# A graph layer in 41 steps instead of 45: 24 dense and 16 gathered tiles in each, count columns placed by each tile's span

## The reference, cut to what matters

```python
h = relu(layernorm(x))
deg = max(count of edges per dst, 1)
w_edge = (deg[src] * deg[dst]) ** -0.5
edge_msg = relu(edge_attr @ W1e + b1e) @ W2e + b2e          # edge_attr: (206250, 64)
agg = segment_sum((h[src] + edge_msg) * w_edge[:, None], dst)
combined = (1 + gin_eps) * h + agg
out = relu(combined @ W1n + b1n) @ W2n + b2n + h
return x + out * rsqrt(mean(out * out) + 1.19e-7) * rms_w
```

## Time and profile before

| | before |
|---|---|
| median of 3 runs | 1078.37 us (1076.29 to 1084.59) |
| the profiled execution | 1070.17 us, its span 1068.3 us |
| PE busy | 956.5 us, 90% |
| weight loads (PEld) | 765.3 us, 72% |
| DVE busy | 914.1 us, 86% |
| ACT busy | 651.4 us, 61% |
| POOL busy | 746.8 us, 70% |
| mean granted clock of PE | 0.993 |
| HBM | 147.95 MB read, 145 GB/s |

### The profile page before, as it was taken

How to read it: one execution, slowest core, us unless ns; L and a number is a source line. 1 busy time by engine, 2 the same in 40 slices (tenths; PEclk the granted TensorE clock), 3 DMA queues, 4 the chain that set the end, 5 groups by cost and what they waited for, 6 DMA issues and landing times. The chain is left out here.

```text
span 1068.3 us, 35619 instructions
## 1 busy us (share of the span) xinstructions
PE 956.5 (90%) x12753; PEld 765.3 (72%) x12753; DVE 914.1 (86%) x4066; ACT 651.4 (61%) x1747; POOL 746.8 (70%) x754
## 2 busy tenths in 40 slices
PE   0333999999999999999999999999999999999985
PEld 0332787887887887777887887787777788788753
DVE  6998988988988988988988988987887898898668
ACT  7972666666665665666666666666566666566435
POOL 2035777777777777777777777777777777777374
PEclk9999999999999999999999999999999999999988
DMA  6035455455554454455454455454455545452473
GB/s 240 15 147 202 145 150 141 139 153 143 142 156 143 138 161 143 133 163 144 123 173 140 129 172 136 131 163 130 141 147 150 143 140 157 141 135 67 157 299 106
DMA packets 57740, 156.99 MB, mean 147 GB/s; under 512 B 16051, under 2 KB 23398, under 8 KB 57184
## 3 DMA queue, kind: packets, MB, share of 16 engines
q1 hardware_dynamic: 33776, 104.43, 29.1%
q0 software_dynamic: 22784, 47.07, 18.8%
q10 hardware_dynamic: 1008, 3.21, 0.9%
HBM read 147.95 MB, written 6.70 MB: 145 GB/s over the span
## 5 line engine op out<-in xcount | busy, mean ns | idle before, releaser
L1065 POOL DMA_INDIRECT arena<-node_rows,idx x712 | 702.3, 986 | 228.9 <-issue 153.3
L1236 ACT ACTIVATE arena<-bank 128x294 f16<-128x294 f32 x900 | 327.2, 420 | 256.2 <-PE bank L1141 239.3
L1226 ACT ACTIVATE arena<-bank 128x512 f32<-128x512 f32 x405 | 222.6, 596 | 105.9 <-PE bank L1091 99.6
L1151 PE MATMUL bank<-t_words,arena 128*128 128x256 f16 x2205 | 276.2, 272 | 0.4 <-DVE arena L1354 0.4
L1291 DVE TENSOR_SCALAR arena<-iota_c,code 128x294 f16<-128x294 f16 x900 | 273.7, 359 | 2.3 <-PE bank L1141 2.3
L1304 DVE SCALAR_TENSOR_TENSOR arena<-iota_h,hi_f,bank 128x49 f32<-128x49 f32 x900 | 184.0, 260 | 77.6 <-PE bank L1106 75.7
L1141 PE MATMUL bank<-arena 128*128 128x294 f16 x900 | 206.2, 307 | 18.8 <-DVE arena L1291 12.4
L1091 PEld LDWEIGHTS bank<-w1e,arena 64*128 64x128 f32 x3240 | 215.6, 190 | 4.7
L1091 PE MATMUL bank<-w1e,arena 64*128 64x128 f32 x3240 | 218.1, 272 | 0.0
L1151 PEld LDWEIGHTS bank<-t_words,arena 128*128 128x128 f16 x2205 | 199.0, 97 | 21.2 <-issue 0.6
L1141 PEld LDWEIGHTS bank<-arena 128*128 128x128 f16 x900 | 101.4, 144 | 83.2 <-issue 37.1
(11 more groups left out here) (210 smaller groups left out, 804.9 us busy)
## 6 DMA issues: line engine op xcount, KB each, us to landing
arena<-in_attr SPq DMA_DIRECT2D x90, 512.0 KB
arena<-low_src SPq DMA_DIRECT2D x47, 652.5 KB, 7.6
arena<-node_rows,idx POOLq DMA_INDIRECT x712
arena<-in_attr SPq DMA_DIRECT2D x45, 128.0 KB
node_rows<-arena SPq DMA_DIRECT2D x1, 3160.5 KB, 8.9
arena<-in_x ACTq DMA_DIRECT2D x7, 448.0 KB, 10.9
arena<-in_x SPq DMA_DIRECT2D x6, 512.0 KB, 12.6
out<-arena SPq DMA_DIRECT2D x12, 224.0 KB
```

Source lines behind the costliest of these rows:

```text
L1065: nc.gpsimd.indirect_dma_start(out=edge_rows[:, u, j, 0:ROW], out_offset=None, in_=table, in_offset=bass.IndirectOffsetOnAxis(ap=idx[:, c, ...
L1151: mm = nc.tensor.matmul(x_sum[:, 0:2 * D], strip[:, u, k, :], T16[:, k, :], start=k == 0, stop=k == NBLK - 1)
L1226: nc.scalar.activation(out.rearrange("p (j o) d -> p o j d", o=2), z[:, :, j0:j0 + n // 2, :], ACT.Relu).then_inc(r_ready, 1)
L1236: nc.scalar.activation(strip[:, u, :, tile * W:tile * W + W], pair_bank[:, j * 512:j * 512 + CW].rearrange("p (k w) -> p k w", w=W), ACT.C ...
```

## The change

**Steps.** `TD` goes from 20 to 24: a step holds 24 dense and 16 gathered tiles, and 41 steps hold the 1612 tiles. There are 10 groups of four, two in each phase. The window is 112 nodes wide for the dense part and 88 for the gathered one.

**Columns.** 24 tiles of six columns would need 144, and a matmul has 128 rows. A tile now takes as many columns of `strip` as it spans targets. POOL works out the starts in the prologue: span of each tile, a running sum over 24, correction, two matrices of 41x984 that PE turns (4 matmuls) and DVE makes into a correction `off[:, 0]` with three operations of 128x984. ACT still writes six columns per tile; the tile after it writes over the surplus, so copies must land in order. Where they go is no longer fixed: ACT loads the starts of a phase's tiles into registers, two loads per phase and two for a step's first pair.

**Places.** In a phase PE counts `FIRST_PAIR[p]`, then the pairs in `MORE_PAIRS[p]`; where there are two of these, the first stands between two halves of the spread. ACT copies the first pair's counts between the two relus. The 49 blocks of the spread are dealt to the phases as 10, 4, 17, 17 and 1. `low_oh` is made for six tiles at a time, four times a step. Row buffers are laid as row, r, row, with one r between two rows.

```diff
-TD, TG = 20, 16
+TD, TG = 24, 16
-LOOKS = [0, 2, 4, 6, 8, 10]
+LOOKS = [0, 2, 4, 6, 9, 12]
-PHASES = [(0, 1), (2, 3), (4, 5), (6, 7), (8,)]
+PHASES = [(0, 1), (2, 3), (4, 5), (6, 7), (8, 9)]
-SPREAD_AT = [0, 10, 12, 27, 42, 49]
+SPREAD_AT = [0, 10, 14, 31, 48, 49]
+FIRST_PAIR = [1, 3, 5, 8, 11]
+MORE_PAIRS = [(2,), (4,), (6, 7), (9, 10), ()]
-LB = 10
+LB = 6
...
+            for by in (1, 2, 4, 8, 16):
+                nc.gpsimd.tensor_copy(widths[:, 1 - a, 0:by], widths[:, a, 0:by])
+                step(nc.gpsimd.tensor_tensor(widths[:, 1 - a, by:TD], widths[:, a, by:TD], widths[:, a, 0:TD - by], ALU.add))
...
+            pool.wait_ge(fast_ready, 1)
...
+            for a, of in ((0, starts[:, 1:TD + 1]), (1, jumps[:, :])):
+                nc.gpsimd.tensor_tensor(spread_out[:, a, :, :], own_step, of.unsqueeze(1).broadcast_to((S, S, TD)), ALU.mult).then_inc(columns_ready, 1)
...
+                    pool.wait_ge(deg_done, 1)
+                    pool.wait_ge(split_in, 16 * 12)
+                    nc.gpsimd.memset(strip_words, 0.0).then_inc(strip_clear, 1)
...
+            v.wait_ge(columns_turned, 1)
+            step(nc.vector.tensor_scalar(passed, bank2[0][:, 0:S * TD], part_f[:, 0:1], None, ALU.is_le))
+            step(nc.vector.tensor_tensor(passed, passed, bank2[1][:, 0:S * TD], ALU.mult))
+            step(nc.vector.tensor_reduce(off[:, 0, :], code[:, :, :], AX.X, ALU.add))
...
             def keep_counts(c, u, p):
                 for j in range(2):
                     act.wait_ge(tile_ps, 2 * (c * NA + p) + (j + 1))
+                    if p > 0:
+                        act.wait_ge(strip_ready, 2 * (c * NA + p - 1) + (j + 1))
-                    nc.scalar.activation(strip[:, u, :, tile * W:tile * W + W],
+                    nc.scalar.activation(strip[:, u, :, bass.ds(column_of[2 * p + j], W)],
...
-                        if p > 0:
-                            keep_counts(c, u, 2 * p)
-                        relu(c, u, 2 * p)
-                        if p < NPH - 1:
-                            relu(c, u, 2 * p + 1)
-                        keep_counts(c, u, 2 * p + 1)
+                        for q in MORE_PAIRS[p - 1] if p > 0 else ():
+                            keep_counts(c, u, q)
+                        load_columns(c, (FIRST_PAIR[p],) + MORE_PAIRS[p])
+                        relu(c, u, PHASES[p][0])
+                        keep_counts(c, u, FIRST_PAIR[p])
+                        relu(c, u, PHASES[p][1])
+                if live(c + 1):
+                    load_columns(c + 1, (0,))
```

More of the change, by code:

```diff
@@ L405, in degree_pass @@
                 mm.then_inc(placed, 1)
+            pe.wait_ge(columns_ready, 2)
+            for a in range(2):
+                numbers_of = spread_out[:, a, :, :].rearrange("p s t -> p (s t)")
+                for n0 in range(0, S * TD, 512):
+                    n1 = min(S * TD, n0 + 512)
+                    mm = nc.tensor.matmul(bank2[a][:, n0:n1], ones[0:S, :], numbers_of[:, n0:n1], start=True, stop=True)
+            mm.then_inc(columns_turned, 1)
             pe.wait_ge(zeros_ready, 1)
@@ L907, in look_of, with phase_of @@
 def look_of(pair):
-    return pair // UL * NPH + pair % UL // 2 + 1
+    return pair // UL * NPH + phase_of(pair % UL) + 1
+def phase_of(k):
+    return sum(k >= first for first in LOOKS[1:])
 def low_set(c, p):
@@ L925, in steps, with encode @@
         one(c, c % 2)
-def encode(nc, part, code, hi_f, rel_d, inside, step):
+def encode(nc, part, code, hi_f, rel_d, wide, inside, step):
     if part == 0:
@@ L934, in encode @@
     if part == 1:
-        step(nc.vector.scalar_tensor_tensor(out=inside, in0=rel_d[:, :, :], scalar=float(W), in1=inside, op0=ALU.is_lt, op1=ALU.mult))
+        step(nc.vector.scalar_tensor_tensor(out=inside, in0=rel_d[:, :, :], scalar=wide[:, 0:1], in1=inside, op0=ALU.is_lt, op1=ALU.mult))
     if part == 2:
@@ L1202, in one @@
                         turn(c - 1)
-                    if live(c) and not last:
-                        count_pair(c, u, 2 * p + 2)
+                    if more:
+                        count_pair(c, u, more[-1])
                     if live(c + 1) and last:
@@ L1227, in relu, with load_columns @@
                                      ACT.Relu).then_inc(r_ready, 1)
+            column_of = {}
+            def load_columns(c, pairs):
+                for j in range(2):
+                    at = j * NA + pairs[0]
+                    _, values = nc.values_load_multi_w_load_instructions(
+                        column_at[c:c + 1, at:at + len(pairs)], engines=(act.engine,), min_val=0, max_val=XS - W,
+                        skip_runtime_bounds_check_because="the prologue takes these columns only where the last one is at most XS - W")
+                    for p, value in zip(pairs, values):
+                        column_of[2 * p + j] = value
             def keep_counts(c, u, p):
@@ L1455 @@
     tile_of_slot = tiles(TILE_D + TILE_G)
-    group_of_slot = tiles([GROUP_AT[g] for g, _ in SLOTS_D] + [TD + GROUP_G[g] for g, _ in SLOTS_G])
     part = _np.arange(128)
```

285 lines of the change are left out of this document (180 added, 105 removed).

## The result

| | before | changed |
|---|---|---|
| median | 1078.23 us (1076.29 to 1084.59) | 1122.59 us (1121.18 to 1122.74) |
| ratio, 95% interval | | 1.0391 [1.0354, 1.0428] |
| span of the profiled execution | 1068.3 us | 1121.0 us |

The change makes the kernel 4% slower. The forecast was 1076 us, and 1122.6 lies outside its range. Of the rivals the third comes nearest: "at 0.25 per phase the step is 23.0 and the total +42".

A forecast was written before the change was run, and what follows sets the result against it. PE was taken to bound the steps, DVE next. Steps -11.3, prologue +7.0, head +3.9, tail and epilogue +0.2 made -0.2 against the profiled 1070.17; from the median 1078.37, less 2 us of lag: 1076 us, range 1061 to 1091.

The forecast's parts named there:

- third rival: ACT's register loads delay each phase's relu; decides from 0.5 us per step, total 1118 or 1092 us; chance 0.08.
- PE's step: Steady step on PE: 20.13 us plus 1.71 of work, -0.2 DVE waits, +0.3 ACT waits, making 21.94.
- DVE's work: Steady step on DVE: 17.5 us grows to 20.5, plus about 0.7 of waits for looks, staying behind PE.
- the lag of POOL: Steady steps: POOL's gathers get a step 1.8 us longer, so their lag and 3.4 us over 44 steps go.
- second rival: DVE becomes the bound, keeping 1.7 us of look waits beside 20.5 of work: step 22.2, total 1090; chance 0.10.
- so I cost them at 0: ACT's 12 register loads per step, issued during a 0.74 us wait for PE: 0; uncovered, up to 3.6 us.
- Copies at 0.73 a pair: ACT's copies of counts in a step: two more pairs, each taking 0.73 us as before the change.
- room on average: ACT in a step: busy 12.4 us grows to 14.4 of some 22, tight only inside phases 2 and 3.
- +0.3 for the middle and last pairs in phases 2 and 3: PE waits there for ACT's copies to free banks: +0.3 us per step, bounds 0 and 0.6.
- Head: First step, bound by DVE, and run-up picking four more tiles in series with looks: +3.9 us, 2 to 5.
- Prologue: DVE's chain: mask delay +4.2, three operations +3.2, longer operations +0.8, degrees -1.2: +7.0 us, 3 to 11.
- The 2 us: Plain runs exceed the profiled execution partly through lagging gathers; that lag goes, taking 2 us off the forecast total.

The follow-up runs named there:

- constant even columns: Changed kernel with dense column starts as even constants in the program, no loads or register operations on ACT, counts in wrong columns: 1081.54 us, ratio 1.0017.

## Why the prediction was wrong, point by point

- **PE's step** came out right, in part by luck. With ACT's two new costs taken away it is 22.03 for 21.94. In that kernel PE is busy 195.58 of 202 us, 21.33 a step where the kernel before has 19.91: +1.42 for the forecast +1.71. Its idle time rose by 0.4 where -0.2 and +0.3 were forecast. The two errors cancel.

```profile
326.00:528.00 202.00, 195.58 (x2779) 160.46 (x2780) 186.72 (x911) 129.58 (x340) 154.26 (x141) 1.00 0.50 145
```

- **DVE's work** (20.5) and the lag of POOL were right. DVE is busy 179.26 / 202 x 22.98 = 20.4 us a step. POOL is no longer full and waits for counts, 43.3 us of 400. PE's waits for DVE's pairs are off the list. DVE's waits for looks did not shrink to 0.7 but are 42.3 of 400 us, 2.4 a step; with constant even columns 28.1, or 1.55. In that kernel 20.4 and 1.55 fill 21.9 of 22.03 us, so whether PE or, as the second rival had it, DVE bounds it is open.
- **"so I cost them at 0"** is the step that failed. The loads were priced at the 303 ns of the earlier trace rows, a load of one value; here 8 of 12 fetch two or three values and take about 500 and 720 ns. Twelve are 6.1 us of ACT's queue, not the 3.6 named as the most. And the cover was one wait of 0.74 us in one phase, applied to all five; phases 2 and 3 load six values, 1.45 us. The register operations were put at nothing too, as covered by the copy before. Price of both: 0.69 us a step, 0.53 with even columns. The third rival, with a chance of 0.08, had its point of decision right, 0.5 us a step, but not its size: 0.25 in each of five phases would be 1.25 and make 23.2, not 23.0. The rule that spoke against the loads, a floor of about 600 ns per load (the Trainium skill, DMA: Bandwidth & Descriptors, "Latency and other measured facts"), is contradicted by the loads of 279 ns; its sum of 7.2 us came out near 6.1 for another reason, the number of values.
- **Copies at 0.73 a pair**: this duration belongs to even columns. The change moves where they land, and the mean rose from 420 to 503 ns. Price: 0.42 us a step, 0.26 without the loads. No rival had it.
- **"room on average"** for ACT compared 14.4 us of busy time with 22, and left the queue's own work out. With it ACT's sum is 22.6 of 22.98.
- **+0.3 for the middle and last pairs in phases 2 and 3** was of the right kind, but sat in the wrong place: PE's recorded waits are for the second relu of phases 1 and 4, at the head of phases 2 and 0, 8.2 us of 400. They come from the order and not from the two costs: with constant even columns they are 8.1.
- **Steps in all**: loads and odd columns together 0.95 x 40 = 38.0 of the 41.6 us missed; the other 3.6 are 0.09 a step.
- **Head**, 5.7 for 3.9: the same two costs. With constant even columns it is 142.7 - 106.4 = 36.3, only 2.7 more than before.
- **Prologue**, 16.0 for 7.0. The check's outcome (`fast`) is there 5.63 us later, 30.36 for 24.73, since `heads` arrives at 16.03 for 9.86. DVE waits 4.86 more for the mask. These were together to cost 4.2. Degrees gave back 1.4 (forecast 1.2). L691 lost 2.92 to the memset, which was costed at nothing ("releases nothing that is needed then"): the lock was overlooked. The three operations and the longer ones came as forecast, 3.2 and 0.8. The sum, 5.63 + 4.86 - 1.4 + 2.92 + 3.2 + 0.8, is 16.0. Why `heads` comes late stays open: with `tails` issued later its cast still started at 15.79. The new load of `slots`, 12.8 KB, took until 12.84 and was not tried at another place.
- **The 2 us** put into the forecast for lag in the plain runs: the guess had the right direction and was too small. Where the kernel before takes 1078 us, its runs spread over 8 to 16 us in each batch (1070.05 to 1086.09 in that of the constant even columns), and the changed kernel's over 1.6; ten runs with constant even columns lie within 0.9. So what makes most runs of the kernel before longer than the profiled one is gone with the change. What it is stays open, since only the one execution of 1070.17 us was traced.
- **3.4 us** "by which 888.9 exceeds 44x20.13" is 3.2; nothing hangs on it.

With both costs gone the kernel ties with the median of the one before (1.0017), but only because most plain runs of that one are slower than its profiled run. Against the profiled execution of the kernel before its span is 11.5 us longer: four steps fewer save 7.7, and prologue, head and tail cost 16.0, 2.7 and 0.5. No version that computes the layer beats the kernel before.

## What to carry to other kernels

Count an engine's queue work (register loads, register operations) as its time: add it to the busy time before you call an engine idle at 60%, and price a load by the values that it fetches. When a change moves only the address of a write, the duration of the write is not safe: look for the alignment that the old addresses happened to have. Work is hidden only by the wait that stands at its own place, so count such waits phase by phase. And a memset on GpSimd isn't free for every DVE operation: here it stretched products with a scalar (L691, L695) and left those of two tensors (L688) alone.

## What the hardware showed that was not expected

- A register load from SBUF on ACT's queue, 492 in the changed kernel's trace: 279 to 313 ns for one value, 480 to 531 for two, 693 to 752 for three, some 215 ns for each further value.
- An f16 copy of 49 runs of six on ACT: 391 to 473 ns at even start columns, 601 to 697 at odd ones, 406 to 455 at odd ones that begin 2 bytes into 16 (five traces with known columns).
- A DVE operation of 82 elements took 3.48 us and one of 28 elements 1.91 beside POOL's memset and product; a POOL operation of 24 elements took 1.90 beside DVE.
